# Attention and norm of an 8-core layer: half of the transposed-probability evictions on VectorE, the feed-forward norm's casts and squares on GpSimd, one wide copy in phase 0

## Chip, cores and metric
The kernel runs on all 8 cores of one Trainium2 chip. Each core computes one batch element of shape 2048 x 1024 by itself; no data passes between cores. The time is the device time of the slowest core, in microseconds (us).

## What is computed
```
xn = layernorm(x)                       # 8 x 2048 x 1024, float32
s  = L0_attn_ref(xn)                    # silu(n@W_hidden), silu(n@W_qk), softmax of q^T k / 2048
                                        # (2048 x 2048 features), its row sums scale v, @ W_out, + xn
g  = silu(L0_ffn_ref(xn))               # two layers of:
    h = shift_token(x)                  #   second half of the features moved one token back
    q, k, v = split(h @ wqkv)           #   8 heads of 64; l2norm, scale, rotary with xpos
    x = x + local_attention(q,k,v) @ wo #   windows of 512 queries, keys of this and the last window,
                                        #   masked to a band of 512 back, softmax
    h = shift_token(x)
    h = (h - mean) / sqrt(var + 1e-5) * lg + lb
    a, gt = split(h @ w1 + b1)
    x = x + (a * gelu(gt)) @ w2 + b2
return x + s * g
```

## The kernel before
Everything is written as tasks in program order. A task names its engine, the tiles it reads and those it writes; the helper works out which earlier tasks it must wait for and puts semaphore waits in front of it. **Each engine carries out its own tasks strictly in the order in which they were written down**; between engines only the waits order anything. `flush` closes a stage: the next one begins when all engines are done with it. DMAs that change the type of the data are issued by GpSimd; in the kernel before GpSimd does nothing else (besides four memsets of constants at the start).

The stages, one after another: phase 0 (`phase0`), the feature-by-feature attention (p1, p2, p3, p4), then for each of two layers: qkv with its norm and rotary chain, local attention (`_local_attn`), output projection, the feed-forward norm (in `ffn_layer`, from line 999), and the two halves of the feed-forward (w1, w2 twice), and at the end the final phase.

**Phase 0** goes over 16 row tiles of 128 tokens. For each: load of x, statistics on VectorE with two small ScalarE steps, XNT, the second statistics, NTB, eight bf16 transposes (`pbf`), eight f32 transposes (`pxf`), the copies of `pbf` on ScalarE (L469), and `ev_x`: eight VectorE copies of 128x128 from PSUM tile `pxf` to `XNW` (L489), which a DMA then writes out. Tile t+1's statistics stand behind `ev_x` of tile t in VectorE's order.

**Local attention** goes over hp (4 pairs of heads), w (4 windows of 512 queries) and it (4 blocks of 128 queries). u is the head within the pair. Window 0 has 128 to 512 key columns per block (`band`), the others 640. The order in which tasks are written down for one turn (one it) is:

```python
for u in range(2): s_task(hp, w, it, u, jt0, iv)  # PE: scores + mask -> pS[u]
if it > 0: emit_tp(hp, w, it - 1)                 # per u: PE transposes -> pPT[u], then eviction to PT[u]
softmax(hp, w, it)   # DVE max u0,u1; ACT exp u0,u1; DVE reciprocal u0,u1; DVE scale u0,u1
```

After the fourth turn come `emit_tp(hp, w, 3)`, the output matmuls (L1437, which need all eight evictions of PT) and the eviction of their result on ScalarE (L1447). `pS` and `pPT` each have one buffer per u, so the scores of the next turn wait for this turn's exponential of the same u. In the names below: scores L1326 and mask L1333, row maximum L1347, exponential L1355, reciprocal L1364, scaling L1371, transposes L1393, eviction of the transposes L1401 (both u on ScalarE).

**The feed-forward norm** works on 8 feature tiles k of 128 x 2048 tokens. First `ABF[k]` = bf16 cast of `XF[k]` (L1018; from k = 4 on shifted by one token, with a one-column memset, L1024 and L1025). Column sums by TensorE with a vector of ones (L1033, which needs all eight casts), the mean spread to all partitions (L1047, L1052), the differences `TDIF[k]` (L1058, eight VectorE instructions of 128x2048), then, for 4 chunks c of 512 tokens and 8 tiles k, the square of 128x512 into one of two buffers `SQS[k % 2]` (L1066, VectorE) and the matmul that adds it up (L1071). Then rsqrt by Ln and Exp on ScalarE, spread, and the normalized tile N2 (L1100, L1104).

Of the kernel before, what the change touches and what calls it, by code (L numbers as in the profile page):

```python
# [10 lines left out]
AF = mybir.ActivationFunctionType  # L11
# [5 lines left out]
NT, DT = N // 128, D // 128  # L17
# [237 lines left out]
class Build:  # L255
# [149 lines left out]
    def phase0(self):  # L405
        nc, p = self.nc, self.p
        h = self.h
        with ExitStack() as S:
# [3 lines left out]
            XNW = S.enter_context(nc.sbuf_tensor("XNW", [128, 2, DT, 128], F32))  # L412
# [11 lines left out]
            for t in range(NT):  # L424
                b = t % 4
# [59 lines left out]
                       writes=(f"pxf{bp}",), tag=f"p0.tpx{t}")  # L485

                def ev_x(e, t=t, b=b, bp=bp):
                    for k in range(DT):
                        mm = e.tensor_copy(XNW[:, bp, k, :],  # L489
                                           pxf[:, bp, k * 128:(k + 1) * 128])  # L490
                    return mm
                p.task("vector", ev_x, reads=(f"pxf{bp}",),
                       writes=(f"XNW{bp}",), tag=f"p0.evx{t}")
                p.dma("gpsimd",
# [290 lines left out]
    def ffn_layer(self, l):  # L785
# [213 lines left out]
        with ExitStack() as S5:  # L999
            N2 = S5.enter_context(nc.sbuf_tensor(f"N2{l}", [128, DT, N], BF16))  # L1000
            self.N2 = N2
            with ExitStack() as S5a:
# [12 lines left out]
                p.dma("sync", FLB[:], h["flb_t"][l], writes=("FLB",), tag=f"f{l}.flb")  # L1015
                for k in range(DT):
                    if k < 4:
                        p.task("vector", lambda e, k=k: e.tensor_copy(  # L1018
                            ABF[:, k, :], XF[:, k, :]),
                            reads=(f"XF{k}",), writes=(f"ABF.{l}{k}",),  # L1020
                            tag=f"f{l}.sh2{k}")
                    else:
                        def shift2(e, k=k):
                            e.memset(ABF[:, k, 0:1], 0.0)  # L1024
                            return e.tensor_copy(ABF[:, k, 1:N], XF[:, k, 0:N - 1])  # L1025
                        p.task("vector", shift2, reads=(f"XF{k}",),
                               writes=(f"ABF.{l}{k}",), tag=f"f{l}.sh2{k}")
                abf_res2 = tuple(f"ABF.{l}{k}" for k in range(DT))
                for c in range(4):
# [33 lines left out]
                for c in range(4):  # L1063
                    sc = c % 2
                    for k in range(DT):
                        p.task("vector", lambda e, k=k, c=c: e.tensor_tensor(  # L1066
                            SQS[:, k % 2, :], TDIF[:, k, c * 512:(c + 1) * 512],
                            TDIF[:, k, c * 512:(c + 1) * 512], op=ALU.mult),
                            reads=(f"TDIF{k}",), writes=(f"SQS{k % 2}",),
                            tag=f"f{l}.sq{c}.{k}")  # L1070
                        p.task("tensor", lambda e, k=k, c=c, sc=sc: e.matmul(  # L1071
                            pst[:, sc, :], self.ones_col[:], SQS[:, k % 2, :],
                            start=(k == 0), stop=(k == DT - 1)),
                            reads=(f"SQS{k % 2}", "ones_col_bf"),
                            writes=(f"pst{sc}",),
                            tag=f"f{l}.vmm{c}.{k}")
                    p.task("scalar", lambda e, c=c, sc=sc: e.activation(
                        LNF[:, c * 512:(c + 1) * 512], pst[:, sc, :], AF.Ln,
                        scale=1.0 / D, bias=self.epsv[0:1, :]),
                        reads=(f"pst{sc}", "epsv"), writes=(f"LNF.{c}",),  # L1080
                        tag=f"f{l}.vln{c}")
# [157 lines left out]
    def _qk_chain(self, l, m, pb, DSTP, QW, SQ, T1, T2, ROWS, RSTDB, ESC,  # L1239
                  psq, pex, pR):  # L1240
        p = self.p
        is_q = m < 4
        mt = m if is_q else m - 4
        er = 0 if is_q else 1
        qw_res = tuple(f"QW{pb}.{c}" for c in range(4))
        for c in range(4):
            p.task("vector", lambda e, c=c, pb=pb: e.tensor_tensor(
                SQ[:, pb, :], QW[:, pb, c * 512:(c + 1) * 512],
                QW[:, pb, c * 512:(c + 1) * 512], op=ALU.mult),
                reads=(f"QW{pb}.{c}",), writes=(f"SQ{pb}",), tag=f"f{l}.sqr{m}.{c}")  # L1250
            p.task("tensor", lambda e, c=c, pb=pb: e.matmul(
                psq[:, pb, :], self.E2Csb[:], SQ[:, pb, :],
                start=True, stop=True),
                reads=(f"SQ{pb}", "E2C"), writes=(f"psq{pb}",),
                tag=f"f{l}.ssq{m}.{c}")
            p.task("scalar", lambda e, c=c, pb=pb: e.activation(
                ROWS[0:2, pb, c * 512:(c + 1) * 512], psq[:, pb, :], AF.Ln),
                reads=(f"psq{pb}",), writes=(f"LNR{pb}.{c}",),
                tag=f"f{l}.l2ln{m}.{c}")
        lnr_res = tuple(f"LNR{pb}.{c}" for c in range(4))  # L1260
        p.task("scalar", lambda e, pb=pb: e.activation(
            ROWS[0:2, pb, :], ROWS[0:2, pb, :], AF.Exp, scale=-0.5),
            reads=lnr_res, writes=(f"LNE{pb}",), tag=f"f{l}.l2ex{m}")
        p.task("vector", lambda e, pb=pb: e.tensor_scalar(
            RSTDB[:, pb, :], ROWS[0:2, pb, :], 1e12, None, op0=ALU.min),
            reads=(f"LNE{pb}",), writes=(f"RSTDB{pb}",), tag=f"f{l}.clip{m}")
        for c in range(4):
            p.task("tensor", lambda e, c=c, pb=pb: e.matmul(
                pex[:, 0, :], ESC[:, er, :], RSTDB[:, pb, c * 512:(c + 1) * 512],
                start=True, stop=True),  # L1270
                reads=(f"RSTDB{pb}", f"ESC{er}"), writes=("pex0",),
                tag=f"f{l}.exp{m}.{c}")
            p.task("vector", lambda e, c=c: e.tensor_tensor(
                QW[:, pb, c * 512:(c + 1) * 512],
                QW[:, pb, c * 512:(c + 1) * 512], pex[:, 0, :], op=ALU.mult),
                reads=("pex0",) + qw_res, writes=(f"QW{pb}.{c}",),
                tag=f"f{l}.qn{m}.{c}")
        dst_res = ("QPf" if is_q else "KPf") + str(mt)
        for c in range(4):
            pe = c % 2  # L1280
            p.task("tensor", lambda e, c=c: e.matmul(
                pR[:, 0, :], self.ROTTsb[:],
                QW[:, pb, c * 512:(c + 1) * 512], start=True, stop=True),
                reads=(f"QW{pb}.{c}", "ROTT"), writes=("pR0",),
                tag=f"f{l}.rot{m}.{c}")
            p.task("vector", lambda e, c=c, mt=mt: e.tensor_tensor(
                DSTP[:, mt, c * 512:(c + 1) * 512], pR[:, 0, :],
                self.ROTsb[:, 1, c * 512:(c + 1) * 512], op=ALU.mult),
                reads=("pR0", "ROT1"), writes=(dst_res,),
                tag=f"f{l}.t2{m}.{c}")  # L1290
            p.task("vector", lambda e, c=c: e.tensor_tensor(
                T1[:, 0, :], QW[:, pb, c * 512:(c + 1) * 512],
                self.ROTsb[:, 0, c * 512:(c + 1) * 512], op=ALU.mult),
                reads=(f"QW{pb}.{c}", "ROT0"), writes=("T10",),
                tag=f"f{l}.t1{m}.{c}")
            p.task("vector", lambda e, c=c, mt=mt: e.tensor_tensor(
                DSTP[:, mt, c * 512:(c + 1) * 512],
                DSTP[:, mt, c * 512:(c + 1) * 512], T1[:, 0, :],
                op=ALU.add),
                reads=("T10", dst_res), writes=(dst_res,),  # L1300
                tag=f"f{l}.rsum{m}.{c}")

    def _local_attn(self, l, QP, KP, VTM, OA, PB, PT, pS, pPT, pO):
# [81 lines left out]
        def emit_tp(hp, w, it):  # L1385
            jlo, W = band(w, it)
            jb0 = jlo // 128
            nb = W // 128
            for u in range(2):
                def ptp(e, u=u, it=it, jb0=jb0, nb=nb):  # L1390
                    for jj in range(nb):
                        jb = jb0 + jj
                        mm = e.transpose(  # L1393
                            pPT[:, u, jj * 128:(jj + 1) * 128],
                            PB[:, it % 2, u, jb * 128:(jb + 1) * 128],
                            self.ident_bf[:])
                    return mm
                p.task("tensor", ptp, reads=(f"PB{u}.{it % 2}", "identity_bf"),
                       writes=(f"pPT{u}",), tag=f"f{l}.tp{hp}.{w}.{it}.{u}")
                def pev(e, u=u, it=it, jb0=jb0, nb=nb):  # L1400
                    return e.activation(  # L1401
                        PT[:, u, jb0:jb0 + nb, it * 128:(it + 1) * 128],
                        pPT[:, u, 0:nb * 128].rearrange("p (a b) -> p a b", b=128),
                        AF.Identity)
                p.task("scalar", pev, reads=(f"pPT{u}",),
                       writes=(f"PTc{u}.{it}",),
                       tag=f"f{l}.pe{hp}.{w}.{it}.{u}")

        def icols(w, jt, njt):
            if w == 0:  # L1410
# [114 lines left out]
```

How the kernel before makes its waits and increments, by code:

```python
                    def _(eng):  # L114
                        cov = self.cov[e]
                        for (deps, emit, dslot, tag) in tasks:
                            for key, val in sorted(deps.items()):
                                if cov.get(key, 0) >= val:
                                    continue
                                if key[0] == "d":
                                    sem = self.dsems[key[1]][key[2]]
                                else:
                                    sem = self.sems[key[1]]
                                eng.wait_ge(sem, val)
                                cov[key] = val
                            if emit is None:
                                continue
                            if dslot is not None:
                                insts = emit(eng)
                                assert len(insts) == 1, tag
                                insts[0].then_inc(self.dsems[e][dslot], 16)
                            else:
                                inst = emit(eng)
                                if inst is None:
                                    inst = eng.nop()
                                inst.then_inc(self.sems[e], 1)
```

## Time and profile before

| | us |
|---|---|
| two runs | 4061.07 and 4107.63, median 4084.35 |
| profiled execution | 4056.7 |
| its slowest core (6), first to last instruction | 4054.9 (cores 4033.1 to 4054.9) |
| TensorE busy | 2736.1 (67%) |
| VectorE busy | 1164.4 (29%) |
| ScalarE busy | 916.0 (23%) |
| GpSimd busy (issuing DMAs) | 204.5 (5%) |
| mean granted TensorE clock, core 6 | 0.770 of full speed |

PE is TensorE, DVE VectorE, ACT ScalarE, POOL GpSimd. A matmul's end in the profile is modelled. Shares over the whole span mix stages with different limits; the rows further down are of single stages. In a timeline row that stands for several instructions (x2, x10) the duration reaches from the first start to the last end.

### The profile page before, as it was taken

How to read it: one execution, taken by the hardware profiler on the slowest of the kernel's cores; microseconds unless marked ns; L12 is line 12 of the kernel's file. 1: busy time of each engine (PE TensorE's matmuls, PEld its weight loads, DVE VectorE, ACT ScalarE, POOL GpSimd, SP SyncE). 2: the span in 40 equal slices, each digit the busy share in tenths (PEclk: the TensorE clock that was granted, in tenths of full speed). 3: DMA queues.
4: the chain of work that ended last, by engine and by line, in shares of the span. 5: the costliest groups of instructions: out<-in, count | busy, mean ns of one | idle time of the engine just before them, and what ended most of it. 6: DMA issues, size and time to landing. Idle time of an engine off the chain costs nothing. (4 is left out here: it accounts for less than half of the span.)

```text
span 4054.9 us, 34778 instructions; the slowest of 8 cores (4033.1 to 4054.9 us)
## 1 busy us (share of the span) xinstructions
PE 2736.1 (67%) x11741; PEld 1170.0 (29%) x11952; DVE 1164.4 (29%) x2221; ACT 916.0 (23%) x1570; POOL 204.5 (5%) x262
## 2 busy tenths in 40 slices
PE   1286567389683566665588998754666666989982
PEld 1222223134231122332133343311332321433432
DVE  3513332101013343333611111243433343111113
ACT  2321111133211214443121010112244412101101
POOL 0000000000000000000011011100000000110110
PEclk7588788789796675555789999866655576999995
DMA  5200000310343100000055555400000002564557
GB/s 122 76 11 1 0 0 1 59 24 1 70 139 103 21 11 11 1 1 11 0 60 63 60 67 59 57 21 11 11 1 1 1 11 32 68 66 57 66 57 249
DMA packets 213604, 170.27 MB, mean 42 GB/s; under 512 B 97573, under 2 KB 193976, under 8 KB 208312
## 3 DMA queue, kind: packets, MB, share of 16 engines
q0 software_dynamic: 200896, 119.59, 21.2%
q1 hardware_dynamic: 12536, 48.44, 4.0%
q8 instruction: 101, 1.65, 0.2%
q14 instruction: 71, 0.58, 0.1%
HBM read 237.26 MB, written 25.17 MB: 65 GB/s over the span
## 5 line engine op out<-in xcount | busy, mean ns | idle before, releaser
L1209 PE MATMUL pa<-N,W1B 128*128 128x512 bf16 x1392 | 337.5, 384 | 72.9 <-DMA W1B<-w1ag 71.8
L1171 PE MATMUL px<-PROD,W2B 128*128 128x512 bf16 x1378 | 321.7, 387 | 50.8 <-DMA W2B<-w2cb 48.8
L606 PE MATMUL psim<-KF,QT 128*128 128x512 bf16 x1004 | 237.0, 398 | 155.8 <-DVE QT L594 154.5
L1221 PE MATMUL pg<-N,W1B 128*128 128x512 bf16 x1364 | 329.0, 380 | 3.8 <-issue 2.5
L1233 DVE TENSOR_TENSOR PROD<-pa,GEB 128x1024 bf16<-128x1024 f32 x88 | 107.8, 1224 | 632.4 <-ACT GEB L1228 632.4
L1326 PE MATMUL pS<-KP,QP 64*128 64x512 bf16 (+2 forms) x448 | 149.9, 418 | 167.9 <-ACT PB L1355 138.8
L1347 DVE TENSOR_REDUCE small<-pS 128x1 f32<-128x640 f32 (+4 forms) x256 | 187.7, 740 | 234.3 <-PE pS L1333 228.4
L890 PE MATMUL pqkv<-ABF,WQKV 128*128 128x512 bf16 x752 | 203.0, 434 | 65.1 <-DMA WQKV<-wqkv 62.0
L1228 ACT ACTIVATE GEB<-pg,B1G 128x1024 bf16<-128x1024 f32 x88 | 98.0, 1114 | 555.7 <-PE pg L1221 555.7
L1401 ACT ACTIVATE PT<-pPT 128x640 bf16<-128x640 bf16 (+4 forms) x256 | 149.6, 634 | 273.4 <-PE pPT L1393 272.8
L1393 PE MATMUL pPT<-ident_bf,PB 128*128 128x128 bf16 x1120 | 144.0, 311 | 99.1 <-DVE PB L1371 99.1
L1209 PEld LDWEIGHTS pa<-N,W1B 128*128 128x128 bf16 x1408 | 138.3, 99 | 243.0 <-issue 82.2
L1171 PEld LDWEIGHTS px<-PROD,W2B 128*128 128x128 bf16 x1408 | 134.7, 99 | 222.1 <-issue 76.3
L1355 ACT ACTIVATE PB<-pS,small 128x640 bf16<-128x640 f32 (+4 forms) x256 | 184.6, 733 | 40.6 <-DVE small L1347 33.8
L606 PEld LDWEIGHTS psim<-KF,QT 128*128 128x128 bf16 x1024 | 103.4, 102 | 289.1 <-issue 179.6
L1221 PEld LDWEIGHTS pg<-N,W1B 128*128 128x128 bf16 x1408 | 123.3, 98 | 165.6 <-issue 41.0
L671 PE MATMUL pv<-ABF,WH 128*128 128x512 bf16 x500 | 121.3, 382 | 64.4 <-DMA WH<-W_hidden 63.6
L1393 PEld LDWEIGHTS pPT<-ident_bf,PB 128*128 128x128 bf16 x1120 | 123.9, 147 | 127.2 <-issue 123.4
L1184 DVE TENSOR_TENSOR XF<-XF,px 128x512 f32<-128x512 f32 x64 | 44.0, 688 | 337.7 <-PE px L1174 337.7
L737 PE MATMUL ps<-VG,WO 128*128 128x512 bf16 x502 | 113.1, 386 | 39.1 <-DMA WO<-W_out 38.6
L1333 PE MATMUL pS<-MSK,ident_bf 128*128 128x128 bf16 (+3 forms) x416 | 139.4, 415 | 0.0
L890 PEld LDWEIGHTS pqkv<-ABF,WQKV 128*128 128x128 bf16 x768 | 83.2, 109 | 181.9 <-issue 116.9
(140 smaller groups left out, 2852.8 us busy)
## 6 DMA issues: line engine op xcount, KB each, us to landing
W1B<-w1ag POOLq DMA_DIRECT2D x88, 512.0 KB, 6.1
W2B<-w2cb POOLq DMA_DIRECT2D x32, 704.0 KB, 7.8
XT<-x SPq DMA_DIRECT2D x16, 512.0 KB, 4.3
xn_scr<-XNW POOLq DMA_DIRECT2D x16, 512.0 KB, 3.9
WH<-W_hidden POOLq DMA_DIRECT2D x8, 1024.0 KB, 30.8
XNB<-xn_scr SPq DMA_DIRECT2D x8, 1024.0 KB, 6.7
s_scr<-SB POOLq DMA_DIRECT2D x8, 1024.0 KB, 8.5
XF<-xn_scr SPq DMA_DIRECT2D x8, 1024.0 KB, 22.8
```

Source lines behind the costliest of these rows:

```text
L606: mm = e.matmul(psim[:, pb, c * 512:(c + 1) * 512], QT2[:, qp, kt, dl:dl + 128], KF[:, kt, c * 512:(c + 1) * 512], start=(kt == 0), stop=( ...
L671: mm = e.matmul(pv[:, sc, :], WH[:, k, hp * 128:(hp + 1) * 128], ABF[:, k, c * 512:(c + 1) * 512], start=(k == 0), stop=(k == DT - 1))
L890: mm = e.matmul(pqkv[:, sc, :], WQKV[:, k, ms * 128:(ms + 1) * 128], ABF[:, k, c * 512:(c + 1) * 512], start=(k == 0), stop=(k == DT - 1))
L1171: e.matmul(px[:, pb, :], W2B[:, s2, k, :], PROD[:, k, cc * 512:(cc + 1) * 512], start=(k == 0), stop=False)
L1209: e.matmul(pa[:, mp, cc * 512:(cc + 1) * 512], W1B[:, sl, k, 0:128], self.N2[:, k, nh0 + cc * 512:nh0 + (cc + 1) * 512], start=(k == 0), s ...
L1221: mm = e.matmul(pg2[:, mp, cc * 512:(cc + 1) * 512], W1B[:, sl, k, 128:256], self.N2[:, k, nh0 + cc * 512:nh0 + (cc + 1) * 512], start=(k ...
L1326: e.matmul(pS[:, u, lo:lo + n], QP[u * 64:(u + 1) * 64, hp, iv:iv + 128], KP[u * 64:(u + 1) * 64, hp, jt0 * 128 + lo:jt0 * 128 + lo + n], ...
L1333: mm = e.matmul(pS[:, u, lo:lo + n], self.ident_bf[:], self.MSKsb[:, it, moff + lo:moff + lo + n], start=False, stop=True)
L1347: p.task("vector", lambda e, u=u, sc=sc, jlo=jlo, W=W: e.tensor_reduce(small[:, sc:sc + 1], pS[:, u, jlo:jlo + W], axis=AX.X, op=ALU.max, ...
L1355: e.activation(PB[:, it % 2, u, jlo:jlo + W], pS[:, u, jlo:jlo + W], AF.Exp, bias=small[:, sc:sc + 1], accum_out=small[:, sc + 1:sc + 2]),
L1393: mm = e.transpose(pPT[:, u, jj * 128:(jj + 1) * 128], PB[:, it % 2, u, jb * 128:(jb + 1) * 128], self.ident_bf[:])
L1401: return e.activation(PT[:, u, jb0:jb0 + nb, it * 128:(it + 1) * 128], pPT[:, u, 0:nb * 128].rearrange("p (a b) -> p a b", b=128), AF.Iden ...
```

## The change
Four edits and two that do nothing:

1. Phase 0: the eight copies of `ev_x` become one copy of 128x1024, on VectorE as before.
2. Feed-forward norm: the eight casts to `ABF` (with four memsets) go from VectorE to GpSimd, in both layers.
3. Feed-forward norm: the 32 squares go from VectorE to GpSimd, in both layers.
4. Local attention: the eviction of `pPT` for u = 1 becomes a `tensor_copy` on VectorE, written down in the same place; u = 0 stays on ScalarE.
5. In `_qk_chain` a name is assigned earlier and an unused one is gone; no instruction changes.

```diff
--- before.py
+++ after.py
@@ -485,10 +485,9 @@
                        writes=(f"pxf{bp}",), tag=f"p0.tpx{t}")
 
                 def ev_x(e, t=t, b=b, bp=bp):
-                    for k in range(DT):
-                        mm = e.tensor_copy(XNW[:, bp, k, :],
-                                           pxf[:, bp, k * 128:(k + 1) * 128])
-                    return mm
+                    return e.tensor_copy(
+                        XNW[:, bp, :, :],
+                        pxf[:, bp, :].rearrange("p (a b) -> p a b", b=128))
                 p.task("vector", ev_x, reads=(f"pxf{bp}",),
                        writes=(f"XNW{bp}",), tag=f"p0.evx{t}")
                 p.dma("gpsimd",
@@ -1015,7 +1014,7 @@
                 p.dma("sync", FLB[:], h["flb_t"][l], writes=("FLB",), tag=f"f{l}.flb")
                 for k in range(DT):
                     if k < 4:
-                        p.task("vector", lambda e, k=k: e.tensor_copy(
+                        p.task("gpsimd", lambda e, k=k: e.tensor_copy(
                             ABF[:, k, :], XF[:, k, :]),
                             reads=(f"XF{k}",), writes=(f"ABF.{l}{k}",),
                             tag=f"f{l}.sh2{k}")
@@ -1023,7 +1022,7 @@
                         def shift2(e, k=k):
                             e.memset(ABF[:, k, 0:1], 0.0)
                             return e.tensor_copy(ABF[:, k, 1:N], XF[:, k, 0:N - 1])
-                        p.task("vector", shift2, reads=(f"XF{k}",),
+                        p.task("gpsimd", shift2, reads=(f"XF{k}",),
                                writes=(f"ABF.{l}{k}",), tag=f"f{l}.sh2{k}")
                 abf_res2 = tuple(f"ABF.{l}{k}" for k in range(DT))
                 for c in range(4):
@@ -1063,7 +1062,7 @@
                 for c in range(4):
                     sc = c % 2
                     for k in range(DT):
-                        p.task("vector", lambda e, k=k, c=c: e.tensor_tensor(
+                        p.task("gpsimd", lambda e, k=k, c=c: e.tensor_tensor(
                             SQS[:, k % 2, :], TDIF[:, k, c * 512:(c + 1) * 512],
                             TDIF[:, k, c * 512:(c + 1) * 512], op=ALU.mult),
                             reads=(f"TDIF{k}",), writes=(f"SQS{k % 2}",),
@@ -1243,6 +1242,7 @@
         mt = m if is_q else m - 4
         er = 0 if is_q else 1
         qw_res = tuple(f"QW{pb}.{c}" for c in range(4))
+        dst_res = ("QPf" if is_q else "KPf") + str(mt)
         for c in range(4):
             p.task("vector", lambda e, c=c, pb=pb: e.tensor_tensor(
                 SQ[:, pb, :], QW[:, pb, c * 512:(c + 1) * 512],
@@ -1275,9 +1275,7 @@
                 QW[:, pb, c * 512:(c + 1) * 512], pex[:, 0, :], op=ALU.mult),
                 reads=("pex0",) + qw_res, writes=(f"QW{pb}.{c}",),
                 tag=f"f{l}.qn{m}.{c}")
-        dst_res = ("QPf" if is_q else "KPf") + str(mt)
         for c in range(4):
-            pe = c % 2
             p.task("tensor", lambda e, c=c: e.matmul(
                 pR[:, 0, :], self.ROTTsb[:],
                 QW[:, pb, c * 512:(c + 1) * 512], start=True, stop=True),
@@ -1397,14 +1395,23 @@
                     return mm
                 p.task("tensor", ptp, reads=(f"PB{u}.{it % 2}", "identity_bf"),
                        writes=(f"pPT{u}",), tag=f"f{l}.tp{hp}.{w}.{it}.{u}")
-                def pev(e, u=u, it=it, jb0=jb0, nb=nb):
-                    return e.activation(
-                        PT[:, u, jb0:jb0 + nb, it * 128:(it + 1) * 128],
-                        pPT[:, u, 0:nb * 128].rearrange("p (a b) -> p a b", b=128),
-                        AF.Identity)
-                p.task("scalar", pev, reads=(f"pPT{u}",),
-                       writes=(f"PTc{u}.{it}",),
-                       tag=f"f{l}.pe{hp}.{w}.{it}.{u}")
+                if u == 0:
+                    def pev(e, u=u, it=it, jb0=jb0, nb=nb):
+                        return e.activation(
+                            PT[:, u, jb0:jb0 + nb, it * 128:(it + 1) * 128],
+                            pPT[:, u, 0:nb * 128].rearrange("p (a b) -> p a b", b=128),
+                            AF.Identity)
+                    p.task("scalar", pev, reads=(f"pPT{u}",),
+                           writes=(f"PTc{u}.{it}",),
+                           tag=f"f{l}.pe{hp}.{w}.{it}.{u}")
+                else:
+                    def pev(e, u=u, it=it, jb0=jb0, nb=nb):
+                        return e.tensor_copy(
+                            PT[:, u, jb0:jb0 + nb, it * 128:(it + 1) * 128],
+                            pPT[:, u, 0:nb * 128].rearrange("p (a b) -> p a b", b=128))
+                    p.task("vector", pev, reads=(f"pPT{u}",),
+                           writes=(f"PTc{u}.{it}",),
+                           tag=f"f{l}.pe{hp}.{w}.{it}.{u}")
 
         def icols(w, jt, njt):
             if w == 0:
```

## Rows read from the trace of the kernel before

**Rows 1.** Busy time in three stretches: phase 0, layer 0's attention, its norm; columns first
```profile
core 6: us, PE busy (x) PEld busy (x) DVE busy (x) ACT busy (x) POOL busy (x), PEclk, DMA share, GB/s
29.00:210.00 181.00, 43.51 (x256) 37.56 (x256) 97.94 (x250) 62.90 (x192) 13.34 (x15) 0.59 0.32 90
1520.00:1922.00 402.00, 243.41 (x1216) 119.37 (x1232) 150.45 (x384) 178.96 (x401) 2.12 (x4) 0.56 0.03 6
...
1958.00:2036.00 78.00, 28.26 (x72) 6.00 (x72) 46.82 (x69) 24.13 (x18) 0.00 (x0) 0.58 0.00 0
```

**Rows 2.** Timeline, one turn of an attention window: start, duration (us), engine, instructions
```profile
1575.65 0.80 ACT L1355 ACTIVATE PB<-pS,small 128x640 bf16<-128x640 f32 x1
...
1576.79 0.69 PE L1326 MATMUL pS<-KP,QP 64*128 64x256 bf16 x2 [1.89 <-ACT PB L1355]
...
1578.22 0.82 DVE L1347 TENSOR_REDUCE small<-pS 128x1 f32<-128x640 f32 x1
...
1579.20 1.27 PE L1393 MATMUL pPT<-ident_bf,PB 128*128 128x128 bf16 x10
...
1580.04 1.30 ACT L1401 ACTIVATE PT<-pPT 128x640 bf16<-128x640 bf16 x2 [2.73 <-PE pPT L1393]
...
1581.23 0.80 ACT L1355 ACTIVATE PB<-pS,small 128x640 bf16<-128x640 f32 x1
```

**Rows 3.** Timeline: two row maxima in a row, and the exponential behind them
```profile
1596.10 1.58 DVE L1347 TENSOR_REDUCE small<-pS 128x1 f32<-128x640 f32 x2 [6.74 <-PE pS L1333]
...
1597.02 0.79 ACT L1355 ACTIVATE PB<-pS,small 128x640 bf16<-128x640 f32 x1 [1.08 <-DVE small L1347]
```

**Rows 4.** Timeline: the last turn of a sequence's first window
```profile
1534.04 0.85 PE L1393 MATMUL pPT<-ident_bf,PB 128*128 128x128 bf16 x6
...
1534.67 0.87 ACT L1401 ACTIVATE PT<-pPT 128x384 bf16<-128x384 bf16 x2 [2.41 <-PE pPT L1393]
...
1535.43 0.69 ACT L1355 ACTIVATE PB<-pS,small 128x512 bf16<-128x512 f32 x1
```

**Rows 5.** Timeline: a window's end, its last transposes and evictions
```profile
1589.21 1.23 PE L1393 MATMUL pPT<-ident_bf,PB 128*128 128x128 bf16 x10 [3.15 <-DVE PB L1371]
...
1590.00 1.30 ACT L1401 ACTIVATE PT<-pPT 128x640 bf16<-128x640 bf16 x2 [1.53 <-PE pPT L1393]
```

**Rows 6.** Groups by line and form: count, busy us, mean ns, idle before
```profile
L469 ACT ACTIVATE ABF<-pbf,lnb_sb,lng_sb 128x128 bf16<-128x128 bf16 x128 | 46.5, 468 | 36.1 <-PE pbf L460 36.1
...
L489 DVE COPY XNW<-pxf 128x128 f32<-128x128 f32 x128 | 26.8, 282 | 48.6 <-PE pxf L480 48.6
...
L1490 DVE TENSOR_TENSOR OT<-XB,pfin 128x1024 f32<-128x1024 f32 x16 | 19.5, 1221 | 41.0 <-DMA out<-OT 36.0 <-PE pfin L1483 5.0
...
L1473 DVE TENSOR_TENSOR XF<-XF,SS 128x2048 f32<-128x2048 f32 x8 | 18.3, 2292 | 17.6 <-DMA SS<-s_scr 17.6
...
L866 DVE COPY VTM<-ptv 128x512 bf16<-128x512 bf16 x32 | 12.0, 418 | 3.0 <-PE ptv L856 3.0
...
L257 POOL MEMSET const-float32-1.0<- 128x1 f32 x1 | 0.1, 99 | 0.0
```

**Rows 7.** Timeline of phase 0: one copy group and what follows it
```profile
40.72 1.68 DVE L489 COPY XNW<-pxf 128x128 f32<-128x128 f32 x8 [3.08 <-PE pxf L480]
...
42.31 0.68 DVE L432 BATCH_NORM_STATS2 ST<-XT 128x6 f32<-128x512 f32 x1
```

**Rows 8.** Timeline of layer 0's norm: casts, differences, squares with their sums
```profile
1958.46 4.63 DVE L1018 CAST ABF<-XF 128x2048 bf16<-128x2048 f32 x4 [0.32 <-PEq L106]
...
1966.46 1.23 DVE L1025 CAST ABF<-XF 128x2047 bf16<-128x2047 f32 x1
...
1980.79 9.18 DVE L1058 TENSOR_TENSOR TDIF<-ABF,MUB 128x2048 bf16<-128x2048 bf16 x8
...
1989.88 0.75 DVE L1066 TENSOR_TENSOR SQS<-TDIF 128x512 bf16<-128x512 bf16 x2
...
2009.87 0.85 DVE L1066 TENSOR_TENSOR SQS<-TDIF 128x512 bf16<-128x512 bf16 x2 [0.48 <-PE pst L1071]
```

## The prediction
> **What bounds the kernel now.** I first split the trace by stage, since the flushes make the stages strictly consecutive and the shares over the whole span say nothing about three of four edits. In the stretches touched no engine is near its limit [rows 1]: in layer 0's attention (402 us) TensorE is busy 243 us at a granted clock of 0.56, ScalarE 179 us, VectorE 150 us; in the norm (78 us) VectorE is busy 47 us, GpSimd not at all; in phase 0 (181 us) VectorE 98 us. So these stages are chains of engines waiting for one another, and what counts is where an instruction stands in a chain, not how busy its engine is. The timeline was read next, for one turn of each chain.
>
> One attention turn lasts 5.58 us, exponential to exponential, and closes like this [rows 2]: 1.14 us from the start of the exponential of u=0 to the first scores that its end allows; 2.41 us for the scores and masks of both u; 0.84 us until the five transposes of u=0 are there; 1.19 us for two evictions on ScalarE, one after the other; then the next exponential. The row maximum of u=0 (1578.22, 0.82 us) lies beside TensorE's work and is finished two microseconds before its exponential is reached. It costs nothing today. The reader is to see two things: ScalarE's second eviction is on the chain (about 0.6 us), and VectorE's maximum is hidden.
>
> **Edit 4, attention: +67 us.** The eviction of u=1 leaves ScalarE, which alone would give back some 0.6 us a turn. But VectorE does its tasks in written order, and there the eviction of the last turn stands *ahead* of both maxima of this turn. It waits for the last transpose, which TensorE does after both scores. So the maxima, ready to run since the scores ended, queue behind it. The new closing of the turn:
> - transposes of both u: start 1579.20, ten in 1.27 us [rows 2]. Half of them is 0.635 us and ScalarE began 0.84 us after the start, so the hand-over takes 0.205 us. VectorE's eviction starts at 1579.20 + 1.27 + 0.205 = 1580.68.
> - its duration: VectorE reads PSUM in 148 ns fixed plus 1.05 ns a column in f32 (282 ns for 128, 1221 ns for 1024), and the bf16 copy of 512 columns from PSUM, with the same kind of strided output, took 418 ns, or 0.527 ns a column above the same 148 [rows 6]. For 640 columns: 0.485 us.
> - two maxima in a row take 1.58 us where one takes 0.82, so the next instruction starts 0.06 us before the last one ends; and the exponential starts 0.10 us after its maximum ends (1596.10 + 0.82 to 1597.02) [rows 3].
> - exponential: 1580.68 + 0.485 - 0.06 + 0.82 + 0.10 = 1582.03, where it was 1581.23. That is 0.80 us later per turn.
>
> This holds for turns it = 1, 2, 3 (only they have an eviction ahead of their softmax) of the full windows: 2 layers x 4 head pairs x 3 windows x 3 = 72, 57.6 us. In the first window the widths are smaller. For it=3 [rows 4]: transposes from 1534.04, 0.85 us, hand-over 0.205, eviction of 384 columns 0.35 - 0.06, maximum of 512 columns 0.69 (0.82 less 128 columns at 1.05 ns), 0.10: 1536.18 against 1535.43, or 0.75. Each turn before it has 128 columns less: maximum -0.13, VectorE's eviction -0.07, transposes -0.11, against -0.21 for the two old evictions (1.30 at 640, 0.87 at 384 columns [rows 2, 4]), so 0.65 and 0.55. Sum 1.95 us x 8 such windows = 15.6 us. A gain stands against it at each window's end, where no maximum is queued: the second eviction now ends at 1591.30 and would end at 1589.21 + 1.23 + 0.18 + 0.485 = 1591.10 [rows 5] (hand-over 0.79 less half of 1.23). 0.2 us x 32 windows = -6.4 us. Together 57.6 + 15.6 - 6.4 = +67 us. The exponential of u=1 is not pushed further: its maximum ends 0.76 us after the first one, when ScalarE becomes free. The eviction price is nearly known, so I give this term +/- 12 us. Nothing waits on ScalarE's freed 0.6 us.
>
> **Edit 1, phase 0: -7 us.** The eight copies hold VectorE for 1.59 us, until the next tile's statistics, which queue behind them [rows 7]; a 1024-column f32 read from PSUM took 1.221 us [rows 6], less 0.06 overlap 1.16. 0.43 us x 16 tiles = -6.9 us. ScalarE's copies of the other transposes lie beside.
>
> **Edits 2 and 3, the norm: +50 us.** No row shows GpSimd computing, so both prices are bounded by other rows.
> - *Casts.* Eight on VectorE take 1958.46 to 1967.69, 9.23 us [rows 8], and TensorE's column sums need all eight. Below: VectorE's own price, no change. Above: the price per column of the 128-column copies, 2.2 ns [rows 6], 4.5 us a cast. I take one column per VectorE cycle, as the f32 multiply of 2048 columns shows, 2.29 us [rows 6], since GpSimd can hardly be credited with VectorE's double rate. 8 x 2.29 = 18.3 us: +9.1 a layer. The four memsets add 0.1 us each [rows 6], +0.4.
> - *Squares.* From 1989.88 to 2010.72, 20.8 us for 32, or 0.65 each, because two buffers pass between VectorE and TensorE [rows 8]. Below: GpSimd at VectorE's price; the pace stays with the buffers, and the first square need no longer stand behind all eight differences (1980.79 to 1989.88) but follows the first one, about 8 us earlier: -8. Above: ScalarE's 468 ns for 128 columns, 3.66 ns a column [rows 6], 1.87 us a square: 59.8 us, +39. I take the 2.2 ns a column of the short copies, 1.13 us a square, which paces the pair alone (two squares 2.26 us, over the buffer's 1.3): 36.2 us, +15.3. The early start I count at nothing: it needs differences on VectorE and squares on GpSimd to run side by side on the same tiles, and no row shows these two engines at work together.
>
> 24.8 us a layer, 50 us for two. What VectorE gets back here is worthless: it waits for the same sums. GpSimd's next DMAs come after the flush, so none is queued behind its new work.
>
> The Trainium skill, GPSIMD Engine Reference, section 3.1, gives 4497 ns for an f32 tensor_tensor of 2048 columns on GpSimd against 2293 ns on VectorE; this trace agrees on the latter (2292 ns), and no run here shows the former. By it a 512-column square would be about 1.12 us, an estimate, and the sum would stay. Its section 4.1 calls one-input operations roughly line-rate, by which the casts would be cheaper than mine. SBUF — State Buffer, section Who interferes with whom, says that a VectorE instruction with two SBUF inputs and a GpSimd one that reads SBUF block each other; by that the early start is lost, as I counted it; no row here shows it.
>
> **Sum.** 67 - 7 + 50 = +110 us on the profiled execution's 4056.7: **4167 us**, 2.7% slower. The median of the two runs shown, 4084, lies between 4061 and 4108; the profiled execution agrees with the lower one.
>
> **Rivals.**
> - *GpSimd is as quick as VectorE and starts early* (both lower bounds): -16 for the norms, sum 67 - 7 - 16 = +44, 4101 us, within 2%. For it: nothing in the trace excludes it. Against: GpSimd would need VectorE's double rate. The point that decides: 2% is 81 us, reached when the norms cost over 21 us together.
> - *GpSimd is much dearer* (upper bounds): (26.8 + 0.4 + 39) x 2 = +132, sum +192, 4249 us. For it: 64 squares each with a hand-over to TensorE and back, of unknown length on this engine. Against: wide tiles spread fixed costs.
> - *The maximum is not delayed* (other side). If VectorE's maximum were done ahead of the eviction, ScalarE's chain would lose one eviction, 0.59 us: 96 x 0.59 = 57, plus 6 at window ends, -63 - 7 + 50 = -20, 4037 us, no slower. For it: ScalarE's evictions are on the chain today. Against: the written order puts `emit_tp` ahead of `softmax`. It decides at the place of L1347 relative to the new copy.
>
> **How the numbers follow.** Chances: main 0.62, dear GpSimd 0.18, quick GpSimd 0.14, undelayed maximum 0.06. The main case alone, with +/- 12 for attention and +/- 12 for the norms, reaches 4143 to 4191. The range 4112 to 4250 leaves out the undelayed maximum and the far end of quick GpSimd, at most 2 in 10. About 2% is what a measurement of this kernel can tell from no change: 0.80 slower (main and dear), 0.18 within, 0.02 faster (an undelayed maximum with quick casts).
>
> **What the new profile would show.** Attention: turns of about 6.4 us; VectorE's new copy near 485 ns, behind it the maximum, and the exponential waiting for L1347's line instead of following ScalarE's second eviction and 128 evictions left on ScalarE instead of 256. Norm: column sums starting about 18.5 us after the first cast instead of 9.4, squares over 36 us, stage about 103 us instead of 78. Phase 0: a copy of 1.22 us, each tile 0.43 us shorter. I am wrong if the attention stages do not grow (the order argument fails) or if the norm grows by under 10 us or over 60 us a layer (the GpSimd prices fail).

## The result

The change makes the kernel slower: the ratio of after to before is 1.0197, with a 95% interval of 1.0138 to 1.0256, or about +80 us (+56 to +104) on 4057. The changed kernel's profiled execution spans 4133.0 us on its slowest core, against 4054.9. (The median over all its executions is 4222 us, because in most of them the cores of one die or of both ran at a lower granted clock; the ratio and all comparisons leave those executions out.) The forecast was 4167 us with a range of 4112 to 4250: the direction and the two causes were right, the sum of 110 us was 30 too high. The forecast also took 2% as the least that can be told from no change, and the measured change lies just on that border.

Where the 78 us between the two profiled spans lie, from the first instruction of one stage to that of the next (core 6 before, core 3 after):

| stage | before | after | difference | forecast |
|---|---|---|---|---|
| phase 0, first copy to end of last | 170.6 | 163.8 | -6.8 | -7 |
| attention, layer 0 / layer 1 | 400.5 / 400.8 | 428.7 / 427.2 | +28.2 / +26.4 | +33.5 each |
| norm, first cast to first w1 matmul, layer 0 / 1 | 86.6 / 86.6 | 104.3 / 101.1 | +17.7 / +14.5 | +24.8 each |
| output projection, layer 0 / 1 | 35.5 / 35.2 | 35.9 / 35.2 | +0.4 / none | none |

These two are the slowest cores of their executions, and a stage differs between cores by some microseconds (layer 0's attention before: 395.4 to 401.0 us). The means over all eight cores say the same: attention +29.5 and +25.2 us, the norms +17.0 and +16.3, phase 0 -6.8, 81 us in all.

The changed kernel, busy time in its three touched stretches: phase 0, layer 0's attention, its norm (columns as in [rows 1]: us, then PE, PEld, DVE, ACT, POOL busy, granted clock, DMA share, GB/s):

```profile
29.00:204.00 175.00, 43.50 (x256) 37.55 (x256) 91.20 (x144) 62.89 (x192) 13.34 (x15) 0.62 0.34 93
1512.00:1941.00 429.00, 252.02 (x1232) 119.64 (x1232) 172.17 (x448) 150.25 (x337) 2.12 (x4) 0.55 0.03 5
1977.00:2081.00 104.00, 32.31 (x72) 6.42 (x72) 29.19 (x24) 24.24 (x18) 56.47 (x48) 0.55 0.07 8
```

Against [rows 1], the attention stage shows how busy shares mislead: ScalarE's busy time fell from 179 to 150 us, VectorE's rose from 150 to 172, both far from full, and the stage got longer.

One attention turn of the changed kernel, timeline (start us, duration us, engine, line, operation, [idle before <- releaser]); it answers [rows 2]:

```profile
1575.36 0.79 ACT L1353 ACTIVATE PB<-pS,small 128x640 bf16<-128x640 f32 x1 [1.16 <-DVE small L1345]
...
1576.49 0.69 PE L1324 MATMUL pS<-KP,QP 64*128 64x128 bf16 x2 [2.56 <-ACT PB L1353]
...
1577.12 0.72 PE L1331 MATMUL pS<-MSK,ident_bf 128*128 128x128 bf16 x2
...
1578.92 1.27 PE L1391 MATMUL pPT<-ident_bf,PB 128*128 128x128 bf16 x10
1579.75 0.70 ACT L1400 ACTIVATE PT<-pPT 128x640 bf16<-128x640 bf16 x1 [2.73 <-PE pPT L1391]
1580.30 0.49 DVE L1409 COPY PT<-pPT 128x640 bf16<-128x640 bf16 x1 [2.39 <-PE pPT L1391]
1580.70 1.55 DVE L1345 TENSOR_REDUCE small<-pS 128x1 f32<-128x640 f32 x2
1581.61 0.79 ACT L1353 ACTIVATE PB<-pS,small 128x640 bf16<-128x640 f32 x1 [1.16 <-DVE small L1345]
```

The turn is now 6.25 us, exponential to exponential, where it was 5.58. VectorE sits idle for 2.39 us until the transposes are there, though the scores of u=0 that its maximum needs are complete at 1577.84, with the mask of L1331, 1.08 us before the transposes start; then copy and maxima follow in the written order, and the exponential waits for L1345. Before, ScalarE's exponential followed its own second eviction with no wait at all [rows 2].

The norm of layer 0 in the changed kernel, timeline; it answers [rows 8]:

```profile
1977.10 7.40 POOL L1017 CAST ABF<-XF 128x2048 bf16<-128x2048 f32 x4 [44.21 <-POOLq L106]
...
1992.12 9.86 PE L1032 MATMUL pst<-ABF,ones_col 128*1 128x512 bf16 x32 [16.19 <-POOL ABF L1024]
...
2006.21 14.23 DVE L1057 TENSOR_TENSOR TDIF<-ABF,MUB 128x2048 bf16<-128x2048 bf16 x8
2007.59 38.72 POOL L1065 TENSOR_TENSOR SQS<-TDIF 128x512 bf16<-128x512 bf16 x32 [15.61 <-DVE TDIF L1057]
2009.61 0.59 PE L1070 MATMUL pst<-SQS,ones_col 128*1 128x512 bf16 x1 [4.30 <-POOL SQS L1065]
2011.59 0.59 PE L1070 MATMUL pst<-SQS,ones_col 128*1 128x512 bf16 x1 [1.39 <-POOL SQS L1065]
...
2028.46 0.59 PE L1070 MATMUL pst<-SQS,ones_col 128*1 128x512 bf16 x1 [0.41 <-POOL SQS L1065]
2029.45 0.58 PE L1070 MATMUL pst<-SQS,ones_col 128*1 128x512 bf16 x1 [0.41 <-POOL SQS L1065]
```

The column sums start 15.0 us after the first cast (9.4 before). The differences, eight in 9.18 us before, now take 14.23 us, and while they run the squares' matmuls come only every 1.98 us; afterwards every 1.0 us. The squares end 40.1 us after the first difference, where they ended after 29.9. The prices by group, which the trace of before could not show (a mean over both layers, so 1245 ns mixes seven squares of about 2 us a layer with 25 of 1.03; 1848 ns mixes differences of 1.22 and 2.06 us):

```profile
L1065 POOL TENSOR_TENSOR SQS<-TDIF 128x512 bf16<-128x512 bf16 x64 | 77.4, 1245 | 30.4 <-DVE TDIF L1057 30.4
...
L1057 DVE TENSOR_TENSOR TDIF<-ABF,MUB 128x2048 bf16<-128x2048 bf16 x16 | 28.5, 1848 | 0.2
...
L1024 POOL CAST ABF<-XF 128x2047 bf16<-128x2047 f32 x8 | 15.0, 1883 | 0.0
L1017 POOL CAST ABF<-XF 128x2048 bf16<-128x2048 f32 x8 | 14.8, 1889 | 84.9 <-POOLq L106 84.9
```

The same groups in the kernel before, on VectorE:

```profile
L1066 DVE TENSOR_TENSOR SQS<-TDIF 128x512 bf16<-128x512 bf16 x64 | 26.9, 425 | 15.1 <-PE pst L1071 15.1
...
L1058 DVE TENSOR_TENSOR TDIF<-ABF,MUB 128x2048 bf16<-128x2048 bf16 x16 | 18.3, 1220 | 0.2
...
L1018 DVE CAST ABF<-XF 128x2048 bf16<-128x2048 f32 x8 | 9.3, 1221 | 0.6 <-PEq L106 0.6
```

### The profile page after: what moved, and what is told of

Read it like the earlier page. It is cut to its first block and busy times, and to the rows that moved or that the text cites. A ratio compares the mean times of both kernels' runs of the same rounds, so it can differ in the third digit from the quotient of the medians.

```text
span 4133.0 us, 34717 instructions; the slowest of 8 cores (4116.3 to 4133.0 us)
## 1 busy us (share of the span) xinstructions
PE 2768.1 (67%) x11952; PEld 1168.9 (28%) x11952; DVE 1166.8 (28%) x2149; ACT 858.5 (21%) x1442; POOL 311.2 (8%) x350
## 5 line engine op out<-in xcount | busy, mean ns | idle before, releaser
L1345 DVE TENSOR_REDUCE small<-pS 128x1 f32<-128x640 f32 (+4 forms) x256 | 179.1, 734 | 142.2 <-PE pS L1331 141.2
L1331 PE MATMUL pS<-MSK,ident_bf 128*128 128x512 bf16 (+2 forms) x448 | 155.9, 433 | 0.0
L1400 ACT ACTIVATE PT<-pPT 128x640 bf16<-128x640 bf16 (+4 forms) x128 | 81.6, 637 | 276.6 <-PE pPT L1391 276.6
```

What stands on the lines that cost most here:

```text
L1331: mm = e.matmul(pS[:, u, lo:lo + n], self.ident_bf[:], self.MSKsb[:, it, moff + lo:moff + lo + n], start=False, stop=True)
L1345: p.task("vector", lambda e, u=u, sc=sc, jlo=jlo, W=W: e.tensor_reduce(small[:, sc:sc + 1], pS[:, u, jlo:jlo + W], axis=AX.X, op=ALU.max, ...
```

## The experiments

Theory: in the attention the delay is one of order (the maxima queue behind the new copy), in the norm it is GpSimd's price per instruction, and VectorE and GpSimd hold each other up when they work side by side. Rivals: the copy on VectorE is costly wherever it stands; ScalarE was never on the chain; the norm alone carries the 80 us; the slow squares come from something other than the neighbour.

**Edit 4 alone** (the last hunk of the diff, nothing else).

> The kernel before with edit 4 alone: the eviction of the transposes of u=1 on VectorE, written ahead of the next turn's maxima. Order theory (the maxima queue behind the new copy): an attention turn of the full windows lasts 6.25 us instead of 5.58, 72 such turns +48 us, 24 turns of the first windows +13 us, 32 window ends -8 us: +53 us, 4110 us, ratio 1.013; both norms keep their 87 us from first cast to first feed-forward matmul. Rival (the attention edit is harmless, the norm carries all of the 80 us): turn of 5.0 to 5.6 us, ratio 1.00 or below.

Measured: 4104.3 us, where the kernel before had a median of 4052.3 on the same chip, or +52 us, 1.3% (from a single execution, so without an interval). Turns of 6.25 us; the attention stage 426.8 and 426.7 us (+26 each, 52 in all; 53 were worked out); the norms unchanged at 85.8 and 87.0 us. So the attention edit makes two thirds of the loss by itself, and the rival that the norm carries it falls.

**The same copy, behind the maxima.** Same instructions, same engines, one task written down later:

```diff
-                    if it > 0:
-                        emit_tp(hp, w, it - 1)
-                    softmax(hp, w, it)
-                emit_tp(hp, w, 3)
+                    late = emit_tp(hp, w, it - 1) if it > 0 else None
+                    softmax(hp, w, it, late)   # calls late() after both maxima
+                emit_tp(hp, w, 3)()
```

(`emit_tp` writes everything as in edit 4, but returns the VectorE task of u=1 as `late` instead of writing it at once.)

> As the run with edit 4 alone, but the VectorE copy of u=1 is written down behind the two row maxima of the next turn instead of ahead of them; instructions and their number are the same. Order theory: the maxima run beside TensorE again, the exponential follows one eviction on ScalarE instead of two, so a turn is 5.58 - 0.59 = 4.99 us; 72 turns -42 us, 24 turns of the first windows -7 us, 32 window ends -8 us: -57 us, 4000 us, ratio 0.986. Rival (a copy from PSUM on VectorE costs the turn whatever its place, by its own time or by slowing the maxima): turn of 6.0 us or more, ratio 1.01. Second rival (ScalarE's evictions were not on the chain): turn stays at 5.58, ratio 1.00.

Measured: ratio 0.9846 (0.9824 to 0.9869), 3988 us. One turn of that kernel, timeline:

```profile
1590.29 1.27 PE L1395 MATMUL pPT<-ident_bf,PB 128*128 128x128 bf16 x10
...
1590.61 0.82 DVE L1347 TENSOR_REDUCE small<-pS 128x1 f32<-128x640 f32 x1 [0.47 <-PE pS L1333]
...
1591.13 0.70 ACT L1404 ACTIVATE PT<-pPT 128x640 bf16<-128x640 bf16 x1 [2.73 <-PE pPT L1395]
1591.67 0.49 DVE L1413 COPY PT<-pPT 128x640 bf16<-128x640 bf16 x1 [0.24 <-PE pPT L1395]
1591.73 0.79 ACT L1357 ACTIVATE PB<-pS,small 128x640 bf16<-128x640 f32 x1
...
1594.13 0.71 PE L1326 MATMUL pS<-KP,QP 64*128 64x128 bf16 x2 [0.36 <-DVE PB L1373]
1594.30 0.83 DVE L1347 TENSOR_REDUCE small<-pS 128x1 f32<-128x640 f32 x1
...
1596.72 0.79 ACT L1357 ACTIVATE PB<-pS,small 128x640 bf16<-128x640 f32 x1
```

The turn is 4.99 us, to the hundredth what the chain gives when one eviction is taken out and none is put in. The copy still takes 0.49 us and still starts about 0.55 us after ScalarE's, but the exponential starts 0.06 us after it instead of 1.31. The maximum (1594.30) again runs beside TensorE's scores of u=1. This settles it: neither the engine nor the duration of the copy costs anything here, its place does, 1.26 us a turn. Both rivals fall.

The stages took 369.0 and 363.0 us on this core, 69 us less than before in all, and 67 us less in the mean of all eight cores, where 57 were expected. The expectation missed something here: it took every full-window turn at 5.58 and 4.99 us. Those are the turns at the lower of TensorE's two clock levels (1.2 of 2.4 GHz, a granted clock of 0.50). Two turns of this kernel, columns as in [rows 1]:

```profile
1591.73:1596.72 4.99, 3.33 (x17) 1.64 (x18) 3.10 (x8) 2.26 (x7) 0.00 (x0) 0.50 0.00 0
1834.22:1837.91 3.69, 1.95 (x17) 1.10 (x18) 2.55 (x8) 2.26 (x6) 0.00 (x0) 1.00 0.00 0
```

At a granted clock of 1.00 the same turn takes 3.69 us. Of the 36 full-window turns of a layer, 9 and 6 were shorter than 5.48 us in the kernel before (core 6; the shortest 4.50, at 0.79), and 8 and 11 shorter than 4.89 in this one, six of them 3.69 us at 1.00. So the mean turn fell by 0.62 us in layer 0 and 0.75 in layer 1, where 0.59 was expected. On core 0 of the kernel before, two turns at 1.00 took 4.28 us, so the order is worth 0.59 us at either level; the rest goes with the clock. Why this kernel was granted the higher level more often is not shown.

**Edit 1 alone.**

> The kernel before with edit 1 alone (one 128x1024 copy in phase 0 instead of eight). My sum: 0.43 us a tile, 16 tiles, -7 us, ratio 0.998. Rival (it also helps or harms the transfers behind it, since the first feed-forward layer starts 10 us earlier in the changed kernel where 7 were expected): the three further us show here too, in the loads behind phase 0.

Measured: ratio 0.9981 (0.9966 to 0.9996), -8 us within an interval of -2 to -14. The sum fits; the few further microseconds by which the first layer started earlier in the changed kernel are inside that interval, and they differ from core to core.

**Edits 1 and 4 with the copy behind the maxima**, casts and squares on VectorE. Two expectations: the second is for a repetition of the same kernel.

> Edit 1 and edit 4 with the copy behind the maxima; casts and squares stay on VectorE. Order theory and additivity: -57 - 7 = -64 us, 3993 us, ratio 0.984. Rival (ratio at or above 1.00) as for the reordered copy.

> The same kernel as the earlier run with edit 1 and the reordered edit 4, casts and squares on VectorE, now timed: its one undisturbed profile spanned 3974 us. Expected 3976 us, ratio 0.980; the difference to the whole change reordered is the price of GpSimd in the norms, 33 us.

Measured: in the first run the eight cores spanned 3959 to 3974 us, and the execution took 3975.7 us; the second gave a median of 3977 us and a ratio of 0.9811 (0.9796 to 0.9825). The first expectation, 3993 us, was 17 too high: the sum had the reordered copy at -57, where its stages gave -67. The kernel beats both others: 1.9% below before, some 3.8% below the changed one.

**The whole change with only the order put right.**

> The whole change, with the VectorE copy of u=1 written behind the two maxima of the next turn; nothing else differs from the changed kernel. Order theory with additivity: attention as in the reordered run (turn 4.99 us, about 366 us a layer), norm as in the changed kernel (101 to 104 us a layer), so -70 for attention, -7 for phase 0, +33 for the norms: 4015 us, ratio 0.989; against the changed kernel -120 us from one moved line. Rival (GpSimd's work in the norm disturbs more than the norm, or the attention gain needs the shorter norm): ratio 1.00 or above.

Measured: ratio 0.9899 (0.9883 to 0.9916), about 4014 us against the 4137 that 1.0197 stands for. Attention 365.3 and 365.5 us on core 5, norms 102.3 and 101.6. So the changed kernel would have been 1% faster than before with one task moved, and the distance to the kernel without GpSimd work, 0.9899 to 0.9811 or 36 us, is the price of edits 2 and 3 (33 us in the norm stages).

**Edit 2 alone (casts).**

> The kernel before with edit 2 alone, the eight casts of the norm on GpSimd. From the changed kernel's 1.88 us a cast, starting 1.85 us apart: first cast to first column sum 15.0 us instead of 9.4, +5.6 us a layer, +11 us in all, 4070 us, ratio 1.003. Rival (GpSimd casts leave TensorE idle so long that the column sums behind them run at the lower clock): up to 3 us a layer more between the first column sum and the first difference.

Measured: ratio 1.0013 (1.0001 to 1.0025), or +5 us (0 to +10), less than the +11 of the stages. The stage itself does what was expected: on core 5

```profile
1944.42 7.40 POOL L1018 CAST ABF<-XF 128x2048 bf16<-128x2048 f32 x4 [41.40 <-POOLq L106]
...
1959.44 9.50 PE L1033 MATMUL pst<-ABF,ones_col 128*1 128x512 bf16 x32 [16.19 <-POOL ABF L1025]
```

15.0 us to the first column sum, norms of 91.6 and 92.1 us where the cores of before had 84.8 to 86.6. From the first column sum to the first difference it is 13.8 us in the mean of cores 4 to 7, where before had 13.4 in the mean (12.9 to 14.2): at most 0.4 us, far from the rival's 3. Why the whole time moved by half of what the norms grew is not settled; single stages vary between cores by up to eight microseconds, for example 395 to 404 us for the attention stages of the kernel before.

**Edit 3 alone (squares).**

> The kernel before with edit 3 alone, the 32 squares of the norm on GpSimd. From the changed kernel: first difference to the end of the last square 40.1 us instead of 29.9, +10.2 us a layer, +20 us in all, 4078 us, ratio 1.005. Within it the seven squares beside the differences take 2 us each and the differences 2.06 us instead of 1.22; the other squares start 1.0 us apart. Rival (the slow squares came from the casts on GpSimd before them): 32 us or less for the squares, and under +4 us a layer.

Measured: ratio 1.0042 (1.0027 to 1.0057), +17 us (+11 to +23). First difference to last square 40.1 us in both layers, differences again 1.85 us in the mean. The norm grew by 10.6 us a layer in the mean of all cores. So the slow squares do not come from casts on GpSimd before them.

**Squares only after all differences** (`reads=(f"TDIF{k}",)` becomes `reads=tdif_res` in the square's task).

> As the run with edit 3 alone, but every square also waits for all eight differences, so the two engines never work side by side. Theory that VectorE's two-input differences and GpSimd's squares block each other: differences back at 1.22 us, all squares at 1.04 us and 1.0 us apart, 9.2 + 0.2 + 32.1 = 41.5 us from first difference to last square, 1.4 us more than side by side; so eight microseconds of earlier start were worth 1.4. Rival (they slow each other only a little and the pace of 2 us is that of the matmuls or of the hand-over): side by side would beat it by 6 us or more, and the first squares stay at 2 us.

Measured, layer 0:

```profile
1999.83 9.17 DVE L1058 TENSOR_TENSOR TDIF<-ABF,MUB 128x2048 bf16<-128x2048 bf16 x8
2009.16 31.99 POOL L1066 TENSOR_TENSOR SQS<-TDIF 128x512 bf16<-128x512 bf16 x32 [73.73 <-DVE TDIF L1058]
```

Differences back at 1.22 us, all 32 squares in 31.99 us, 41.3 us from first difference to last square. Starting eight microseconds early is worth 1.2 us. (This kernel and the next were not timed often enough to compare whole times, 4094 and 4052 us from one comparable execution each; the argument uses the stage alone.) Side by side the two engines take nearly the sum of their times: a difference and a square, 1.15 and 1.0 us apart when alone, come in pairs every 1.98 us, 0.17 less than the sum. In the changed kernel GpSimd has no idle time between these squares: each one lasts up to 2.02 us by itself, and each difference beside it 2.06. It is the instructions that get longer, not a wait between them.

**Casts split between the two engines**, even k on VectorE, odd on GpSimd:

> The kernel before with the four odd casts of the norm on GpSimd and the four even ones on VectorE. If the two engines work side by side: GpSimd's four at 1.86 us end after 7.5 us and the column sums start 1.9 us earlier than before, at 7.5 us instead of 9.4. If a VectorE cast at two columns a cycle and a GpSimd cast block each other: four pairs of 1.16 + 1.86, 12.1 us, 2.7 us later than before, and casts of 3 us are seen on one engine or both.

Measured, layer 0:

```profile
1948.84 4.72 POOL L1018 CAST ABF<-XF 128x2048 bf16<-128x2048 f32 x2 [41.62 <-POOLq L106]
1948.85 5.79 DVE L1018 CAST ABF<-XF 128x2048 bf16<-128x2048 f32 x2 [0.32 <-PEq L106]
1953.55 2.84 POOL L1025 CAST ABF<-XF 128x2047 bf16<-128x2047 f32 x1
1954.57 2.90 DVE L1025 CAST ABF<-XF 128x2047 bf16<-128x2047 f32 x1
...
1960.45 9.39 PE L1033 MATMUL pst<-ABF,ones_col 128*1 128x512 bf16 x32 [12.78 <-DVE ABF L1025]
```

Casts that take 1.22 us on VectorE alone and 1.88 us on GpSimd alone take 2.9 and 2.84 us together. With half the work on each engine the column sums start 11.6 us after the first cast, 2.2 later than with all of it on VectorE. That is near the blocking theory's 12.1 and far from the 7.5 of engines side by side. TensorE is idle through all eight casts, so it has no part in this. The pairs come every 2.83 us, 0.18 less than the 1.16 + 1.85 of the two engines alone.

The Trainium skill, SBUF — State Buffer, section Who interferes with whom, has both pairs: a VectorE cast in a two-port mode contends with GpSimd, and so does a VectorE instruction with two SBUF inputs with a GpSimd one that reads SBUF; it calls the shared pair of ports an exclusive lock, held in the two-port modes for the whole instruction. Both pairs measured here agree with it but for the 0.17 and 0.18 us by which a pair is shorter than the sum. The runs show the engines' times, not the ports.

## Why the prediction was right, and where its sizes were off

- **Attention: the mechanism right, the term of 67 too large: 55 measured in the stages, at the edge of the +/- 12.** The mis-sized step is the closing of the turn, 0.80 us, which was 0.67. I took over ScalarE's hand-over of 0.205 us for VectorE; VectorE's copy starts 1580.30 - 1578.92 - 1.27 = 0.11 us after the last transpose. The copy was 0.49 us as worked out (0.485), the maximum started 0.40 us after it (0.425 taken), and 0.91 us later came the exponential (0.92). In the first windows the turns grew by 0.44, 0.52 and 0.62 us, where 0.55, 0.65 and 0.75 stood. At the window's end 0.26 us came back, not 0.2 (the output matmuls start 2.23 us after the transposes of [rows 5], and 1.97 us after them in the changed kernel). 72 x 0.67 + 8 x 1.58 - 32 x 0.26 = 52.6 us. The other 2 us come from a term that the prediction put at nothing: it took all 72 turns at 5.58 us, but those at a higher granted clock are shorter (15 of 72 before, 13 of 72 after). In the mean of all 72 a turn grew by 0.73 us, 4.4 us more than 72 x 0.67, and the window ends gave back 2.3 us more than 32 x 0.26.
- **Phase 0: right.** 0.43 us a tile, 6.8 us for all.
- **Norm: direction right, 50 where 32 came, outside the +/- 12.** Casts: 2.29 us was taken, 1.88 measured and 1.85 apart, so +5.6 us a layer instead of +9.5; the reason given, that GpSimd can hardly be credited with more than one column per VectorE cycle, was wrong for casts: 1.88 us is 0.92 ns a column, where the prediction's f32 rows give VectorE 1.05. Squares: 1.13 us was taken from the price per column of a 128-column VectorE copy, 1.0 us apart was measured, 32.0 us for 32 instead of 36.2. That it came so near was luck: more than half of such a copy is the fixed part (148 of 282 ns), which says nothing of GpSimd. Counting the early start at nothing was nearly right, but for a reason that the trace of before could not give: it was worth 1.2 us of 8. The squares of the changed kernel did take over 36 us from first to last, 38.7, as forecast, but as seven slow ones and 25 quick ones. First difference to last square: 15.3 us more was forecast, 10.2 measured.
- **The range.** Both large terms were too high, so their errors added up. 4137 us, which the ratio stands for, lies below the 4143 to 4191 of the main case; it is in the whole range because that reached down toward the case of a quick GpSimd.
- **The page's figures.** By the Trainium skill's GPSIMD Engine Reference, section 3.1, whose price is for f32 and 2048 columns, a square was estimated at 1.12 us, and 1.03 to 1.04 us was measured; its section 4.1 calls one-input operations roughly line-rate, and the cast of 2048 columns took 1.88 us, clearly less than my 2.29. For the casts the page would have been the better guide.
- **The rivals.** GpSimd as quick as VectorE: false, by 1.88 to 1.22 us a cast and 1.03 to 0.42 us a square. GpSimd much dearer: false; the hand-over to TensorE disappears behind two buffers. The undelayed maximum: false of this change and true of the moved copy; I priced it at 0.59 us a turn, and 0.59 is what it gave.

## What to carry to other kernels

Moving an instruction to a less busy engine is decided by what stands behind it in that engine's written order, not by the busy shares: ask which ready instruction will now wait behind the moved one's input, and write the moved one after it. Here the same copy on the same engine changed a turn by +0.67 or by -0.59 us. And before giving VectorE's work to an idle GpSimd, ask whether VectorE runs beside it: if so the two may take turns, and the overlap that was to pay for the slower engine is not there.

## What the runs showed of the hardware that I had not expected

- VectorE and GpSimd casts from SBUF, started together, took 2.9 and 2.84 us each instead of 1.22 and 1.88; working side by side gained 0.18 us a pair.
- A `tensor_tensor` of 128x512 bf16 on GpSimd takes 1.03 us alone and up to 2.02 us beside VectorE's two-input subtractions, which themselves go from 1.22 to 2.06 us.
- The first VectorE reader of TensorE's output started 0.11 us after the modelled end of the last transpose, ScalarE's 0.2 us after the middle one. I had treated them as equal.
- The same attention turn of the reordered kernel took 4.99 us at a granted clock of 0.50 and 3.69 us at 1.00, though no engine is near its limit in that stage: TensorE's work is part of the chain.
